# Attention and mixture-of-experts kernel: projections ahead of both score parts, except in one unit of eight

## What is computed

```python
q = (Q @ Wq_w + Wq_b).reshape(b, tq, H, DK).transpose(0, 2, 1, 3)
k = (K @ Wk_w + Wk_b).reshape(b, tk, H, DK).transpose(0, 2, 1, 3)
v = (V @ Wv_w + Wv_b).reshape(b, tk, H, DK).transpose(0, 2, 1, 3)
scores = jnp.einsum('bhqd,bhkd->bhqk', q, k) / jnp.sqrt(jnp.float32(DK))
scores = jnp.where(mask == 0, jnp.float32(-1000000000.0), scores)
attn = jax.nn.softmax(scores, axis=-1)
out = jnp.einsum('bhqk,bhkd->bhqd', attn, v)
...
x = x + _L0_xattn_ref(_layernorm(x, axis=-1), ctx_1024, ctx_1024, mask_1x1xSxS2_ik0, ...)
x = x + _L0_ffn_ref(_layernorm(x, axis=-1), L0_ffn_gate_w, L0_ffn_experts_gate_up, L0_ffn_experts_down, ...)
```

## Time and profile before

| | before |
|---|---|
| median of 3 runs | 790.56 us (788.26 to 790.91) |
| the profiled execution | 788.83 us, span 787.0 us |
| granted TensorE clock, mean over the span | 0.987 |
| PE busy | 736.9 us (94%) |
| DVE busy | 534.4 us (68%) |
| ACT busy | 396.1 us (50%) |
| POOL (GpSimd) busy | 348.3 us (44%) |

### The profile page before, as it was taken

The page is one execution under the profiler, slowest core; times in us unless marked ns, Lnnn a source line. Parts: engine busy times, 40 slices in busy tenths (PEclk is TensorE's granted clock), DMA queues, the critical chain, the costliest instruction groups (busy, mean ns, idle before and its releaser), DMA issues.

```text
span 787.0 us, 22011 instructions
## 1 busy us (share of the span) xinstructions
PE 736.9 (94%) x8171; PEld 463.6 (59%) x8171; DVE 534.4 (68%) x1142; ACT 396.1 (50%) x679; POOL 348.3 (44%) x520
## 2 busy tenths in 40 slices
PE   4789999999999999998989889899999999998998
PEld 3545555555556565554456446677777777755655
DVE  6766688888988989887656777433333333358897
ACT  4225566666666666766644553344444444433331
POOL 6152134466665555566575260111122111267774
PEclk9879999999999999999999999999999999999999
DMA  6744555555554455557341232798899989634743
GB/s 181 190 141 145 180 162 161 140 152 173 155 163 151 149 151 141 160 160 207 98 143 55 81 136 54 155 155 179 159 169 172 163 172 164 151 114 128 240 149 114
DMA packets 164234, 118.26 MB, mean 150 GB/s; under 512 B 108450, under 2 KB 143522, under 8 KB 164132
## 3 DMA queue, kind: packets, MB, share of 16 engines
q1 hardware_dynamic: 145844, 79.65, 42.4%
q0 software_dynamic: 10272, 28.88, 12.2%
q10 hardware_dynamic: 8016, 8.33, 3.3%
HBM read 52.78 MB, written 38.14 MB: 116 GB/s over the span
## 4 chain that ended last, share of the span: by engine, by line
PE 63%; DVE 17%; DMA 6%; issue 5%; ACT 4%; POOL 2%; SPq 2%; DVEq 0%; ACTq 0%; POOLq 0%
PE ps_st L1924 16%; PE ps_m L1939 9%; PE ps_st L1495 7%; PE ps_st L1133 6%; DVE mx L1023 5%; PE ps_o L1184 5%; PE ps_m L1207 4%; PE ps_st L1152 2%; PE ps_o L1506 2%; DMA qk_scratch<-arena 2%; PE ps_m L1343 2%; PE ps_st L1168 2%; PE ps_m L1506 2%; PE ps_m L1283 2%; ACT p L826 1%
## 5 line engine op out<-in xcount | busy, mean ns | idle before, releaser
L1023 DVE TENSOR_REDUCE mx<-ps_st 128x4 f32<-128x1024 f32 x128 | 155.6, 1217 | 31.0 <-PE ps_st L1152 23.8
L826 ACT ACTIVATE p<-ps_st 128x1024 f32<-128x1024 f32 x128 | 131.0, 1024 | 76.3 <-PE ps_st L1168 73.5
L1924 PE MATMUL ps_st<-fwh,p 128*128 x568 | 137.9, 313 | 2.3 <-DMA p<-expert_rows 2.3
L1696 POOL DMA_DIRECT2D sorted_out<-p x71 | 38.4, 541 | 181.7 <-ACT p L1753 178.1
L1427 POOL DMA_INDIRECT expert_rows<-hrow,slot x64 | 64.8, 1012 | 75.3 <-DVE slot L1418 55.2
L1924 PE MATMUL ps_st<-fwl,p 128*128 x284 | 88.8, 313 | 0.0
L1924 PEld LDWEIGHTS ps_st<-fwh,p 128*128 128x128 f16 x568 | 55.4, 98 | 29.6 <-issue 3.1
L1133 PE MATMUL ps_st<-maskq,identb 64*64 64x512 bf16 x512 | 52.8, 403 | 15.9 <-DVE mx L1023 13.0
L1495 PE MATMUL ps_st<-q,arena 128*128 128x512 f16 x264 | 59.7, 380 | 4.6 <-DVE qk L1806 2.5
L1495 PE MATMUL ps_st<-qk,arena 128*128 128x512 f16 x264 | 61.2, 387 | 1.7 <-DVE qk L941 1.6
L1753 ACT ACTIVATE p<-ps_m 128x256 f32<-128x256 f32 x71 | 27.3, 384 | 70.3 <-PE ps_m L1939 68.2
(11 more groups left out here) (235 smaller groups left out, 1769.1 us busy)
## 6 DMA issues: line engine op xcount, KB each, us to landing
sorted_out<-p POOLq DMA_DIRECT2D x71, 128.0 KB, 3.0
qk_scratch<-arena SPq DMA_DIRECT2D x32, 256.0 KB, 2.6
arena<-ffn_dram SPq DMA_DIRECT2D x15, 544.0 KB
qk<-qk_scratch SPq DMA_DIRECT2D x44, 128.0 KB, 3.0
arena<-ctx_dram SPq DMA_DIRECT2D x16, 256.0 KB
hT_dram<-hT ACTq DMA_DIRECT2D x16, 256.0 KB, 2.3
out_dram<-xr SPq DMA_DIRECT2D x16, 256.0 KB, 3.3
xr<-x_dram SPq DMA_DIRECT2D x7, 512.0 KB, 4.2
```

The costliest lines, as they stand in the source:

```text
L826: eng.activation(expo[n % 4][:, :, :], ps_st[pair["T", n]][:, :].rearrange("p (h q) -> p h q", h=4), ACT.Exp, scale=SCALE).then_inc(s_e, 1)
L1023: eng.tensor_reduce(mx[b % 2][:, qt, :].rearrange("p (h g j) -> p h g j", h=2, g=HG)[:, :, hg, :], ps_st[pair["S", 8 * b + n]][:, :].rearr ...
L1696: eng.dma_start(sorted_out[k * P:(k + 1) * P, :], ys[k % 3][:, :]).then_inc(r_st[k % 3], 16)
L1924: last = mm(o[:, 0:INTER], xgT[k % NXG][:, xl, dc, :], (fwh, fwl)[wl][:, bass.ds(e, 1), w0 + dc * INTER:w0 + (dc + 1) * INTER], start=dc = ...
```

## The change

On PE, in a unit that has both S and T, the order becomes ring, S, T, V, except for u = 0 (`mt` and `rt` both have slot 0), where it becomes S, T, ring, V. Units with only S or only T keep their order. On ACT, in the units u = 0 with both, the exponential is issued ahead of the copy of `mt`; everywhere else the ACT order stays. On DVE nothing moves; in the router's unit of batch 0 one wait for the end of `logits` is added before the bank is given free.

```diff
@@ scalar
+                    s, st, pv = units(i, u)
+                    turned_first = s and st and u in (slots["mt"], slots["rt"])
+                    if turned_first:
+                        exponential(st)
                     for kind, b in uses(i, u):
...
-                    _, st, pv = units(i, u)
-                    if st:
...
+                    if st and not turned_first:
+                        exponential(st)
@@ vector
                             if b:
                                 places(eng, link, moe, bank((kind, b)))
+                            else:
+                                eng.wait_ge(s_sub, 1)
                             eng.nop().then_inc(free((kind, b)), 1)
@@ tensor
-                    if s:
+                    ahead = s and st and u % 8 not in (slots["mt"], slots["rt"])
+                    if s and not ahead:
                         scores(*s)
+                    if s and st and not ahead:
+                        scores_t(*st)
                     for kind, b in uses(i, u):
...
-                    if st:
+                    if ahead:
+                        scores(*s)
+                    if st and (ahead or not s):
                         scores_t(*st)
```

More of the change, by code:

```diff
@@ L734, in shared_high, with exponential @@
                 eng.activation(f_hi[n % 2][rows, c, :], hf[k % 2][rows, :], ACT.Copy).then_inc(moe.f_hh, 1)
+            def exponential(st):
+                n = 8 * st[0] + st[1]
+                eng.wait_ge(s_st, n + 1)
+                if n >= 4:
+                    eng.wait_ge(s_pv, (n - 4) // 2 + 1)
+                if n == 3:
+                    eng.wait_ge(s_gl, 1)
+                eng.activation(expo[n % 4][:, :, :], ps_st[pair["T", n]][:, :].rearrange("p (h q) -> p h q", h=4), ACT.Exp,
+                               scale=SCALE).then_inc(s_e, 1)
             def values_out(b):
```

## The result

The changed kernel takes 813.04 us as the median of 4 runs (811.32 to 815.88), the kernel before 790.73 beside it: ratio 1.0272 (95% interval 1.0237 to 1.0307). The forecast was slower, by 6 us; it is slower by 22, outside the range of 791 to 802. The profiled execution is 812.63 us, its span 810.8 against 787.0, 23.8 us more.

What follows compares the result with a forecast made beforehand. The prediction took PE's order of blocks as the bound. Block order 5.8, iteration 16 -0.5 and transfers +0.5 gave 5.8, say +6 us: 794.8 us profiled, 796.5 us as median, range 791 to 802.

Steps and rivals of the forecast that it cites:

- What bounds the kernel: PE's order of blocks is the bound: PE at work 94% of the span, DVE 68%, an iteration 22.24 us.
- The gain, 0.12 us for each adjacency: On PE, S and T side by side save 0.12 us; five more adjacencies save 0.60 us an iteration.
- Rivals A and B: PE's shape changes worth more: 0.17 to 0.21, 791 to 793.5 us, chance 0.12; or 0.29, 786 us, chance 0.10.
- the rule set against the rows: The skill's drain of some 175 ns per PE tiling-mode change: 0.88 us saved an iteration, change costing about 2.5 us.
- The price, S to S 1.96: S blocks start at least 1.96 us apart; stalls 1.02 (units 7 to 0), 0.38 (1 to 2), 0.20 (5 to 6).
- just level: At unit 7's reduction, DVE would be ready at 23.49 against 23.43 us for S plus 0.68.
- the step on the order of the blocks: Iterations 4 to 15 take 22.72 us instead of 22.24: 12 x 0.48 = 5.8 us more.
- DVE needs 5.64 from the reduction of unit 5 to that of unit 7: DVE's stretch between these reductions was taken from the kernel before as 5.64 us, 0.20 of it waiting.
- Rival C: DVE becomes the bound, its chain 0.3 to 0.5 us later each iteration: +10 to +12, 800 to 803 us, chance 0.17.
- Transfers: Late transfers stay late in four iterations; the new wait at S of unit 0 adds +0.5 us (0 to 1.5).
- Iteration 16: No projections there; ht fills PE's wait for unit 5's maximum, the wait behind o returns at mt: -0.5 us.

Runs made afterwards that it cites:

- e1: Changed kernel with GpSimd's four low-half subtractions issued later, behind the power of the second layer norm: 800.72 us beside 793.18, ratio 1.0125.
- e2: Changed kernel with GpSimd's four low-half subtractions made memsets at the same place, low halves left out of the result: one run, 795.46 us.
- e13: Changed kernel with GpSimd's power of the first layer norm ahead of the low halves instead of behind: 805.19 us beside 793.0, ratio 1.0151.

## Why the prediction was wrong, point by point

- **What bounds the kernel**: right for the kernel before. PE's order bounds, and DVE is close behind. In the changed kernel PE waits for DVE, mostly from unit 6 to unit 0.
- **The gain, 0.12 us for each adjacency**: right. S and T side by side take 1.00 us in all units (242.95 to 243.95). Rivals A and B, for which a change of shape is worth 0.17 to 0.29, fall, and so does the rule set against the rows: no block after is shorter than the lengths I used.
- **The price, S to S 1.96**: right at units 1 to 2 and 5 to 6. At units 7 to 0 it is 2.05 without GpSimd's interference, 0.09 more, where I had DVE "just level". The iteration was to take 22.72 and takes 22.85 in e1. Over iterations 4 to 15, 12 x 0.48 = 5.8 us was the forecast; e1 against before has 6.0. So the step on the order of the blocks was sized right, in part by luck: a plain iteration is 0.6 longer and not 0.48, but e1 has fewer late transfers than the kernel before in this stretch.
- **The step that failed** is "DVE needs 5.64 from the reduction of unit 5 to that of unit 7". I took DVE's chain as a length that moves along with its start. It isn't: one instruction in it depends on what GpSimd does at that moment. Before, V of unit 4 is followed at once by S of unit 5, and the product runs beside GpSimd's `onl`. After, v stands between the two. The product comes 4.84 us behind V of unit 4 (before 3.23), but GpSimd's subtractions only 4.42 (before 4.06), since that chain starts from ACT's copies behind V of unit 4. So the product now meets the next item of GpSimd's queue, the four subtractions. The chain takes 6.84, and this costs 9.5 us. Rival C had the right place and sign (DVE's chain late, each iteration pays it again, +10 to +12), but named no such cause and had 0.17 of the chance.
- **Transfers**: "+0.5 us (0 to 1.5)" was too small for iteration 3, where S of unit 0 waits 2.70 us against 1.04. e1 has the same order and there an iteration of 21.58, against 23.40 and before 21.26, so it isn't the order's doing alone. In e1, e2 and e13 this S waits 1.73, 1.55 and 1.87 us; why it is 2.70 here wasn't tried.
- **Iteration 16**, -0.5 us forecast, +2.2 measured. In it T of unit 6 waits 1.15 us for the exponential, behind copies on ACT, and then the clock falls:

```profile
383.00:385.50 2.50, 1.06 (x24) 0.53 (x24) 2.33 (x11) 1.71 (x3) 2.22 (x5) 1.00 1.01 332
385.50:389.00 3.50, 3.50 (x32) 1.59 (x25) 0.91 (x3) 1.46 (x2) 3.19 (x6) 0.51 0.14 36
```

  V and o, 2.6 us at the upper level (0.99 and 1.63), take 4.2 there. I had no term for the clock at all; before, it is 1.00 throughout that iteration. The wait of T belongs to the order: e2, with the same order on PE, has it too (1.14). But the clock stays up there, and its iteration 16 takes 19.56, only 0.6 more than before. In e13 (21.17) the clock falls behind this wait as here; in e1 (21.20) it falls earlier in the iteration, 0.72 over 362 to 368 us, and not behind the wait of 1.01. So some 0.6 are the order, and 1.6 a fall of the clock that came in three of these four runs; what decides is open.
- The sum of what was found: 6.0 (order) + 9.5 (GpSimd) + 0.65 (iteration 4, clock) + 2.2 (iteration 16, with the clock) + 2.6 (iterations 2 and 3, transfer and clock) are 20.9 of the 23.8; 1.85 lies ahead of the change and 1.1 behind the attention. About 3 us of it, an estimate, are the clock: 0.65, 1.6, and 0.9 for S and T in iteration 3 (1.85 against 0.99).

## What to carry to other kernels

A reordering on one engine shifts the others against each other. Before summing block lengths, look at what GpSimd and DVE do at the same time in the new order: a DVE instruction with two SBUF operands that slides from beside one GpSimd item to beside the next can grow from 0.3 to 2.3 us. For every buffer that is written again check the distance between its two producers in the new order, for all of them (here 1.96 us for the maxima, 1.76 for the exponentials), and at the edges of the pattern too, since a merge that wins 0.12 us in each unit loses all of it at one uncovered edge.

## What the runs showed of the hardware that was not expected

- A 16-column DVE product waits 2.3 us for a run of four GpSimd subtractions and 2.9 us for a run of eight shorter ones, until the last is done, in most iterations; in a few, in the tensor-and-scalar form, and beside the two instructions of `onl` (0.27 us), it gets in between two of them.
- The same run as memsets, which read nothing, holds it not at all (0.17 us).
- Waits of PE of 0.2 to 1.5 us close together, or one of 2.70, were followed by stretches at the lower clock level: granted 0.50 or 0.51 over 3 to 7 us, in which V lasts 1.7 to 1.9 us and not 0.99 where it lies in them (nearly) whole. It isn't certain: T of unit 6 waits in iteration 16 of four runs, and such a stretch follows in two of them (waits of 1.15 and 1.16, the changed kernel and e13) and not in the others (1.14 and 1.01, e2 and e1).
